# A transformer block on one core: value products of a head group in one burst, seven exponential buffers, three staging buffers

## The chip, the core and the metric
One core of a Trainium2 chip runs the whole program. The metric is the device time of one execution in microseconds. The kernel before takes 591.67 us (median of three runs: 591.47, 597.71, 591.67).

## The reference
Eight sequences of 512 tokens, 128 channels, float32. Layer 1, on the layer-normed x: RMS norm; q, k, v by three 128x128 products; q and k normalised per head (16 heads of 8 channels); scores with a relative-position bias that is constant beyond 128 positions; a causal softmax that excludes the diagonal; values; an output projection with residual; RMS norm; a two-layer ReLU network of 512 hidden units with residual. The result is layer-normed and added to x. Layer 2: layer norm, then eight experts of 352 hidden units, of which each token takes its two best, layer norm and residual.

```python
attn = jnp.einsum('bqhd,bkhd->bhqk', q, k) + bias
attn = attn * scale[None, :, None, None]
attn = jnp.where(causal[None, None], attn, -1000000.0)
attn = jax.nn.softmax(attn, axis=-1)
y = jnp.einsum('bhqk,bkhd->bqhd', attn, v).reshape(B, S, E)
y = y @ Wo + x
...
g = jnp.einsum('th,eih->tei', x, gate_w)
u = jnp.einsum('th,eih->tei', x, up_w)
y = jnp.einsum('tei,ehi,te->th', jax.nn.silu(g) * u, down_w, w_te)
```

## The kernel before
**Stages.** After a start of some 39 us the attention stage runs eight bodies, b = 0 to 7, one per sequence. Then the expert stage runs 71 tiles of 128 tokens (`step` of each engine), the first forty of them interleaved with the end of body 7's work ("bodies" 8 and 9), then a final normalisation.

**A body** has 20 score units, n = 0 to 19, in four groups g of four heads, five units u each. A unit computes transposed scores into one half of the two-part PSUM tile SC (lines 716 to 742): units 0 and 1 take the first key tile of two heads each, units 2 and 3 the second and fourth tile, unit 4 the third tile of four heads. ScalarE takes the exponential of a unit, 128x1024 (line 1015), into a buffer EB[u]. VectorE and GpSimd (POOL) multiply parts of it by an exponential bias table (lines 442 to 455 and 1363): VectorE units 0, 2 and 4, POOL units 1 and 3; in odd bodies from 3 on VectorE takes unit 1 too from the second group on (`takes`). TensorE then multiplies by the values, four heads side by side in 32 columns each, accumulating in the PSUM tile OA (line 748): `pv01` for units 0 and 1, `pv23` for 2 and 3, `pv4` for 4.

**Order.** Every engine works through its queue in the order of the program. That order is written by hand: the dictionaries PE_AT, ACT_AT, DVE_AT and POOL_AT (lines 43 to 50) say behind which unit n of a body a piece of other work is issued. Such work is, for the body ahead, the preparation of q, k, v (`pre_xt`, `pre_qk`, `pre_val`, `pre_turn`, `peel` on TensorE, with the copies `pre_copy` and `first_part` to `third_part` on ScalarE; negative entries lie in the body before the last), and for the body behind, `on_m1`: vsum, o0, o1, yt, wo, zt, h0 to h3, ffn, and the routing (rx, logits, and in odd bodies from 3 on count). These share two PSUM tiles in turn. In odd bodies VectorE runs the routing chain `top`, `second_best` in unit 3, `shares` in 5 and `place` in 6 (line 1446), which waits for count; in bodies 5 and 7 the slot table follows (`expert_tiles`, `past_starts`). POOL's scatters wait for `place`.

**Waits.** Scores of unit n wait for the exponential of unit n-2 (line 721). The value products of group g stand at these places of TensorE's order: `pv01(g)` behind the scores of the group's unit 4, `pv23(g)` behind those of unit 1 of the next group, `pv4(g)` behind those of its unit 2 (lines 962 to 969). The exponential of a unit waits until its buffer of the group before has been multiplied (lines 1012 to 1014).

**Weights.** Twenty lots of expert weights are loaded into seven staging buffers WST (which lie in the later gather buffers YSA, XGA and in WSX), transposed by TensorE (`weights`, line 852) and copied by ScalarE (line 438): lots 0 to 6 behind units 14 to 20 counted from the start of body 6, lots 7 to 19 behind units 3 to 15 of body 7. The load of lot i waits for the transposition of lot i-7 (line 527). On SyncE's queue lots 0 to 6 stand before body 7's stores of q and k, lots 7 to 10 before the loads of the second half of its q and k (lines 553 and 558), the rest behind these. The zero pads of the expert slots are made in XGA and WSX at the start and written out behind body 0's loads (line 578).

Of the kernel before, what the change touches and what calls it, by code (L numbers as in the profile page):

```python
# [71 lines left out]
def block_kernel(nc, x_d, ln1_d, wq_d, wk_d, wv_d, rel_d, scale_d, wo_d, ln2_d, w1_d, w2_d,  # L72
# [30 lines left out]
    with ExitStack() as ctx:  # L103
# [16 lines left out]
        EB = [arena[:, 17408 + 1024 * u:17408 + 1024 * (u + 1)] for u in range(UNITS)]  # L120
# [97 lines left out]
        WSX = sb("WSX", [P, 3 * 512])  # L218
# [223 lines left out]
        def mul_first(eng, g, u):  # L442
            e = EB[u].rearrange("p (j c) -> p j c", j=2)
# [6 lines left out]
        def mul_mid(eng, g, u):  # L450
            e = EB[2 + u].rearrange("p (j c) -> p j c", j=2)
# [42 lines left out]
        def _(sp):  # L494
# [87 lines left out]
            for i in range(NHI + 4, NWT):  # L582
                stage(i)
# [48 lines left out]
        def _(pe):  # L632
# [119 lines left out]
            def pv01(b, g):  # L752
# [8 lines left out]
                e = lambda q0, n: lambda j: EB[j // 2][:, 512 * (j % 2) + q0:512 * (j % 2) + q0 + n]  # L761
# [3 lines left out]
            def pv23(b, g):  # L765
# [3 lines left out]
                e = lambda c, n: lambda j: EB[2 + j // 2][:, 512 * (j % 2) + c:512 * (j % 2) + c + n]  # L769
# [487 lines left out]
        def _(dve):  # L1257
# [287 lines left out]
            for b in range(NB + 2):  # L1545
                at = DVE_AT[b >= NB]
                for n in positions(b):
# [50 lines left out]
                    if 1 <= b <= NB:  # L1598
# [110 lines left out]
        def _(pool):  # L1709
# [90 lines left out]
            for b in range(NB + 2):  # L1800
                at = POOL_AT[b >= NB]
                for n in positions(b):
                    g, u = divmod(n, UNITS)
                    if b < NB and (u == 3 or u == 1 and not takes(b, g)):
# [94 lines left out]
```

## Time and profile before

| | |
|---|---|
| median of three runs | 591.67 us |
| profiled execution | 596.4 us span; its own time is 597.71 us, the only one of the three above the span, so 1.3 us lie around it |
| attention stage (39 to 368 us) | 329 us |
| TensorE / VectorE / ScalarE / POOL busy | 532.1 / 375.9 / 395.4 / 349.7 us |
| mean granted TensorE clock | 0.977 |

Busy time is a share of the span and averages over stages with different limits. Matmuls are pipelined and their records overlap, so the steps between starts tell more than the sum of the durations. Where a line of the trace merges several instructions (x3), its start is that of the first.

### The profile page before, as it was taken

How to read it: one execution, taken by the hardware profiler on the slowest of the kernel's cores; microseconds unless marked ns; L12 is line 12 of the kernel's file. 1: busy time of each engine (PE TensorE's matmuls, PEld its weight loads, DVE VectorE, ACT ScalarE, POOL GpSimd, SP SyncE). 2: the span in 40 equal slices, each digit the busy share in tenths (PEclk: the TensorE clock that was granted, in tenths of full speed). 3: DMA queues.
4: the chain of work that ended last, by engine and by line, in shares of the span. 5: the costliest groups of instructions: out<-in, count | busy, mean ns of one | idle time of the engine just before them, and what ended most of it. 6: DMA issues, size and time to landing. Idle time of an engine off the chain costs nothing.

```text
span 596.4 us, 14609 instructions
## 1 busy us (share of the span) xinstructions
PE 532.1 (89%) x4952; PEld 395.0 (66%) x4969; DVE 375.9 (63%) x1095; ACT 395.4 (66%) x880; POOL 349.7 (59%) x449
## 2 busy tenths in 40 slices
PE   6989899899899899988899899999976899999981
PEld 5655455556566455655555666889976899999960
DVE  6824583965975947996847877527742365555347
ACT  3388989888978788869788696644531355555425
POOL 6104636545538885357877258487578555565545
PEclk9999999999999999999999999999996799999997
DMA  7245333213213322232734512212122203321174
GB/s 196 76 126 161 111 99 109 74 37 108 80 45 122 102 86 71 77 100 78 201 109 134 132 56 52 59 55 69 55 61 69 55 32 86 88 63 32 33 287 141
DMA packets 47016, 55.62 MB, mean 93 GB/s; under 512 B 7376, under 2 KB 41056, under 8 KB 44784
## 3 DMA queue, kind: packets, MB, share of 16 engines
q1 hardware_dynamic: 42624, 45.76, 26.7%
q0 software_dynamic: 4320, 8.92, 4.5%
q8 instruction: 42, 0.69, 0.5%
q14 instruction: 30, 0.25, 0.2%
HBM read 36.27 MB, written 18.92 MB: 93 GB/s over the span
## 4 chain that ended last, share of the span: by engine, by line
PE 56%; DVE 15%; ACT 10%; POOL 6%; issue 6%; DMA 3%; another core or an unknown queue 3%; DVEq 1%; SPq 0%; ACTq 0%; POOLq 0%
PE SC L871 11%; PE OA L748 9%; PE OA L881 6%; PE M L786 4%; PE M L822 4%; PE SC L730 3%; ACT arena L1015 3%; PE SC L734 2%; PE M L643 2%; DVE SS L1330 2%; PE SC L740 2%; PE M L662 1%; POOL slots L1782 1%; PE M L852 1%
## 5 line engine op out<-in xcount | busy, mean ns | idle before, releaser
L1015 ACT ACTIVATE arena<-SC 128x1024 f32<-128x1024 f32 x160 | 161.9, 1039 | 14.7 <-PE SC L735 11.8
L871 PE MATMUL SC<-arena 128*128 128x128 f32 (+1 forms) x852 | 111.5, 283 | 0.0
L871 PEld LDWEIGHTS SC<-arena 128*128 128x128 f32 (+1 forms) x852 | 104.0, 191 | 0.4 <-issue 0.3
L748 PE MATMUL OA<-arena 128*32 128x256 f32 (+1 forms) x1536 | 88.9, 349 | 6.6 <-DVE arena L455 2.8
L1782 POOL DMA_INDIRECT slots<-XBA,IDX x64 | 72.6, 1134 | 37.0 <-DVE IDX L1455 19.6
L1503 DVE TENSOR_TENSOR arena<-arena,SC 128x256 f32<-128x256 f32 (+1 forms) x142 | 43.7, 348 | 68.6 <-issue 24.6
L881 PE MATMUL OA<-arena 128*128 (+1 forms) x426 | 62.5, 284 | 12.9 <-issue 8.1
L748 PEld LDWEIGHTS OA<-arena 128*32 128x32 f32 x1536 | 39.2, 109 | 44.0 <-issue 22.8
L881 PEld LDWEIGHTS OA<-arena 128*128 128x128 f32 (+1 forms) x426 | 55.2, 198 | 15.4 <-issue 15.4
L454 POOL TENSOR_TENSOR arena<-arena 128x512 f32<-128x512 f32 x32 | 42.7, 1335 | 36.2 <-ACT arena L1015 35.6
L447 POOL TENSOR_TENSOR arena<-arena 128x512 f32<-128x512 f32 x23 | 31.2, 1356 | 48.9 <-ACT arena L1015 48.8
L1793 POOL DMA_INDIRECT ytok<-YSA,XGA x39 | 38.7, 993 | 34.0 <-ACT YSA L1118 28.3
L1112 ACT ACTIVATE arena<-SC 128x256 f32<-128x256 f32 (+1 forms) x142 | 38.6, 324 | 25.6 <-PE SC L871 16.6
L1363 DVE TENSOR_TENSOR arena<-arena 128x1024 f32<-128x1024 f32 x32 | 40.6, 1268 | 17.6 <-ACT arena L1015 17.6
L1511 DVE COPY arena<-arena 128x704 f32 x71 | 38.2, 538 | 16.6 <-issue 14.4
L1793 POOL DMA_INDIRECT ytok<-arena x32 | 32.0, 1001 | 27.4 <-ACT arena L1118 23.2
L447 DVE TENSOR_TENSOR arena<-arena 128x512 f32<-128x512 f32 x41 | 34.1, 833 | 18.8 <-ACT arena L1015 18.2
L734 PE MATMUL SC<-arena 72*128 72x384 bf16 x128 | 35.2, 329 | 6.9 <-ACT arena L1015 6.9
L730 PE MATMUL SC<-arena 72*128 72x512 bf16 x128 | 38.4, 381 | 2.9 <-ACT arena L1015 1.3
L1118 ACT ACTIVATE YSA<-OA,XGA 128x128 f32<-128x128 f32 x39 | 14.3, 367 | 36.4 <-PE OA L881 18.9
L454 DVE TENSOR_TENSOR arena<-arena 128x512 f32<-128x512 f32 x32 | 26.1, 816 | 18.3 <-ACT arena L1015 18.2
L1118 ACT ACTIVATE arena<-OA,arena 128x128 f32<-128x128 f32 x32 | 11.8, 367 | 33.0 <-PE OA L881 21.3
(244 smaller groups left out, 1086.0 us busy)
## 6 DMA issues: line engine op xcount, KB each, us to landing
arena<-parts SPq DMA_DIRECT2D x90, 192.0 KB
parts<-arena SPq DMA_DIRECT2D x16, 384.0 KB
arena<-ytok SPq DMA_DIRECT2D x8, 512.0 KB, 7.3
XGA<-slots SPq DMA_DIRECT2D x39, 65.0 KB
arena<-slots SPq DMA_DIRECT2D x32, 65.0 KB, 1.9
X<-in_L_attn_x SPq DMA_DIRECT2D x4, 512.0 KB, 5.1
out<-X SPq DMA_DIRECT2D x8, 256.0 KB, 2.5
arena<-parts SPq DMA_DIRECT2D x12, 96.0 KB
```

Source lines behind the costliest of these rows:

```text
L447: return eng.tensor_tensor(v, v, tab, ALU.mult)
L454: return [eng.tensor_tensor(a, a, TAB[:, h0:h0 + 3:2, P:3 * P], ALU.mult), eng.tensor_tensor(z, z, TAB[:, h0:h0 + 3:2, P:2 * P], ALU.mult)]
L730: mm = pe.matmul(s[:, 512 * i:512 * i + 512], KS[0:ROWS, h, 0:P], QS[0:ROWS, h, :], start=True, stop=True)
L734: pe.matmul(s[:, 512 * i:512 * i + 384], KS[0:ROWS, h, P:2 * P], QS[0:ROWS, h, P:4 * P], start=True, stop=True)
L748: mm = pe.matmul(OA[32 * j:32 * j + 32, q0:q0 + n], vals[:, t, 32 * h:32 * h + 32], probs(j), start=first, stop=last, skip_group_check=True)
L871: mm = pe.matmul(SC[0:n, r % 2, 512 * m + P * c:512 * m + P * (c + 1)], WSEL[s % 4][:, I * m + i0:I * m + i0 + n], XGT[r % 2], start=True, ...
L881: mm = pe.matmul(OA[:, 0:P], HTB[r % 2][0:n, P * c:P * (c + 1)], WALL[0:n, bass.ds(off + 2 * I + P * c, P)], start=c == 0, stop=c == NIC - 1)
L1015: act.activation(EB[u], SC[:, n % 2, :], ACT.Exp).then_inc(exp_done, 1)
L1363: dve.tensor_tensor(e, e, TAB[:, heads, P:3 * P], ALU.mult).then_inc(mul_dve, 1)
L1503: ins = dve.tensor_tensor(HTB[r % 2][0:k, c0:c1], SGB[r % 2][0:k, c0:c1], SC[0:k, r % 2, 512 + c0:512 + c1], ALU.mult)
L1782: pool.indirect_dma_start(out=slots_d.ap(), out_offset=bass.IndirectOffsetOnAxis(ap=IDX[b // 2 % 2][:, k, T * r + t:T * r + t + 1], axis=0 ...
L1793: pool.indirect_dma_start(out=ytok_d.ap(), out_offset=bass.IndirectOffsetOnAxis(ap=XG[r][:, D + 1:D + 2].bitcast(I32), axis=0), in_=YS[r], ...
```

## The change
- `pv01`, `pv23` and `pv4` of group g are issued one after the other, behind the scores of unit 1 of the next group. Only the last group of the last body keeps `pv01` behind its own unit 4, and the other two at the start of the expert stage.
- The exponentials go round a ring of seven buffers (the five of before, a new tile EBX, and YSA) instead of one buffer for each unit of a group. The wait names the unit that had the buffer seven exponentials ago.
- The first gather buffers move from XGA into WSX. Weight lots are staged in the three parts of WSX. On SyncE's queue lots 0 to 2 stand in the first place, 3 to 6 in the second, 7 to 19 in the third. The pads are made in XBA, and VectorE waits for their transfers before it first writes there.
- Places: val from 1 to 2 and qk0 from -4 to -3 on TensorE, qk0 from -5 to -3 on ScalarE, count from 6 to 7 on TensorE; place2, tab0 and tab1 from 6 to 7 on VectorE.

```diff
-PE_AT = (dict(val=1, turn0=4, turn1=8, xt=-5, qk0=-4, qk1=-2, ... count=6, peel00=5, peel01=6, peel10=9, peel11=10),
+PE_AT = (dict(val=2, turn0=4, turn1=8, xt=-5, qk0=-3, qk1=-2, ... count=7, peel00=5, peel01=6, peel10=9, peel11=10),
-ACT_AT = (dict(val=2, seed=1, xt=-6, qk0=-5, qk1=-2, ...
+ACT_AT = (dict(val=2, seed=1, xt=-6, qk0=-3, qk1=-2, ...
-DVE_AT = (dict(... place=5, place2=6, tab0=6, tab1=6, tab2=9, ln=16, xstat=16, xb=19),
+DVE_AT = (dict(... place=5, place2=7, tab0=7, tab1=7, tab2=9, ln=16, xstat=16, xb=19),
...
-        EB = [arena[:, 17408 + 1024 * u:17408 + 1024 * (u + 1)] for u in range(UNITS)]
...
-        XGA = sb("XGA", [P, INNER * ROW])
+        EBX = sb("EBX", [P, 1024])
         YSA = sb("YSA", [P, INNER * D])
+        EBR = [arena[:, 17408 + 1024 * u:17408 + 1024 * (u + 1)] for u in range(UNITS)] + [EBX[:, :], YSA[:, :]]
+        NEB = len(EBR)
+        WSX = sb("WSX", [P, 3 * 512])
+        XGA = WSX[:, 0:INNER * ROW]
...
-        WST = [a[:, 512 * k:512 * (k + 1)] for a, n in ((YSA, 2), (XGA, 2), (WSX, 3)) for k in range(n)]
+        WST = [WSX[:, 512 * k:512 * (k + 1)] for k in range(3)]
         NST = len(WST)
-        PADV = [a[:, 0:E * ROW].rearrange("p (e c) -> p e c", c=ROW) for a in (XGA, WSX)]
+        PADV = [XBA[:, r].rearrange("p t k c -> p (t k) c") for r in range(2)]
...
+        def eb(b, g, u):
+
+            return EBR[(NU * b + UNITS * g + u) % NEB]
...
                 if b == NB - 1:
                     sp.wait_ge(dummy_out, 32)
-                    for i in range(NHI):
+                    for i in range(NST):
                         stage(i)
...
                     if b == NB - 1 and half:
-                        for i in range(NHI, NHI + 4):
+                        for i in range(NST, NHI):
                             stage(i)
...
-            for i in range(NHI + 4, NWT):
+            for i in range(NHI, NWT):
                 stage(i)
...
                     before = (b, g - 1) if g else (b - 1, GROUPS - 1)
-                    if 0 <= before[0] < NB and (b < NB or before[0] == NB - 1 and b == NB and g == 0):
-                        if u == 1 and b < NB or n == 0 and b == NB:
-                            pv23(*before)
-                        if u == 2 and b < NB or n == 0 and b == NB:
-                            pv4(*before)
-                    if b < NB and u == 4:
+                    if b < NB and u == 1 and before[0] >= 0:
+                        pv01(*before)
+                    if b < NB and u == 1 and before[0] >= 0 or b == NB and n == 0:
+                        pv23(*before)
+                        pv4(*before)
+                    if b == NB - 1 and n == NU - 1:
                         pv01(b, g)
...
             def exp_unit(b, n):
-                u = n % UNITS
                 act.wait_ge(qk_done, NU * b + n + 1)
 
-                done = 3 * (GROUPS * b + n // UNITS) + (-2, -2, -1, -1, 0)[u]
-                if done > 0:
-                    act.wait_ge(pv_done, done)
-                act.activation(EB[u], SC[:, n % 2, :], ACT.Exp).then_inc(exp_done, 1)
+                old = NU * b + n - NEB
+                if old >= 0:
+                    act.wait_ge(pv_done, 3 * (old // UNITS) + (1, 1, 2, 2, 3)[old % UNITS])
+                act.activation(eb(b, *divmod(n, UNITS)), SC[:, n % 2, :], ACT.Exp).then_inc(exp_done, 1)
...
                         if n == at["xb"]:
                             dve.wait_ge(x1_rstd, c + 1)
-                            if c >= 2:
+                            if c < 2:
+                                dve.wait_ge(dummy_out, 32)
+                            else:
                                 dve.wait_ge(scattered[c % 2], 16 * 2 * T * (c // 2))
```

## Rows read from the trace of the kernel before

**Rows 1.** Stretches of the span: length, busy time of each engine, granted clock, DMA share.
```profile
39.00:368.40 329.40, 301.51 (x3078) 185.70 (x3093) 234.56 (x581) 274.93 (x494) 196.59 (x192) 1.00 0.33 98
```

**Rows 2.** The same view: body 2 and body 5.
```profile
113.00:153.00 40.00, 37.48 (x364) 22.97 (x366) 27.03 (x66) 35.13 (x63) 20.95 (x21) 1.00 0.25 80
237.90:282.30 44.40, 40.07 (x382) 24.89 (x384) 38.28 (x110) 35.14 (x65) 24.20 (x27) 1.00 0.26 84
```

**Rows 3.** Timeline of TensorE, body 2: start, duration, line, output from input, count.
```profile
137.61 0.64 PE L748 MATMUL OA<-arena 128*32 128x256 f32 x8
138.18 2.05 PE L786 MATMUL M<-W,H1T 128*128 128x128 f32 x16
...
142.88 1.07 PE L748 MATMUL OA<-arena 128*32 128x256 f32 x16
143.88 0.61 PE L730 MATMUL SC<-arena 72*128 72x512 bf16 x2
144.32 0.60 PE L643 MATMUL M<-IDN,arena 128*128 128x128 f32 x4
```

**Rows 4.** Timeline of TensorE at the start of the expert stage.
```profile
373.27 1.51 PE L748 MATMUL OA<-arena 128*32 128x256 f32 x32
374.71 0.66 PE L828 MATMUL M<-IDN,XBA 128*128 128x128 f32 x4
```

**Rows 5.** Timeline of ScalarE, body 4, units 10 to 13; in brackets idle time before.
```profile
218.73 1.02 ACT L1015 ACTIVATE arena<-SC 128x1024 f32<-128x1024 f32 x1
...
220.11 1.11 ACT L1102 ACTIVATE H1T<-M 128x512 f32<-128x512 f32 x2
221.10 1.04 ACT L1015 ACTIVATE arena<-SC 128x1024 f32<-128x1024 f32 x1
222.59 1.02 ACT L1015 ACTIVATE arena<-SC 128x1024 f32<-128x1024 f32 x1 [0.45 <-PE SC L735]
...
225.58 1.02 ACT L1015 ACTIVATE arena<-SC 128x1024 f32<-128x1024 f32 x1 [0.32 <-PE SC L735]
```

**Rows 6.** Timeline of ScalarE, exponentials around and in body 2.
```profile
112.06 2.93 ACT L1015 ACTIVATE arena<-SC 128x1024 f32<-128x1024 f32 x3
...
131.24 1.04 ACT L1015 ACTIVATE arena<-SC 128x1024 f32<-128x1024 f32 x1
...
143.16 1.01 ACT L1015 ACTIVATE arena<-SC 128x1024 f32<-128x1024 f32 x1
...
152.09 2.02 ACT L1015 ACTIVATE arena<-SC 128x1024 f32<-128x1024 f32 x2
```

**Rows 7.** Timelines of TensorE and VectorE, body 3, units 4 to 7.
```profile
164.46 0.60 PE L730 MATMUL SC<-arena 72*128 72x512 bf16 x2
164.98 1.08 PE L748 MATMUL OA<-arena 128*32 128x256 f32 x24
...
167.55 1.90 PE L838 MATMUL M<-MM,ONES 128*128 128x64 f32 x16
...
167.29 1.22 DVE L1363 TENSOR_TENSOR arena<-arena 128x1024 f32<-128x1024 f32 x1
```

**Rows 8.** Timelines of ScalarE and TensorE: idle times in bodies 4 and 5.
```profile
199.25 0.31 ACT L1044 ACTIVATE RSQ<-SS 128x128 f32<-128x128 f32 x1 [2.00 <-DVE SS L1332]
...
215.95 1.07 PE L748 MATMUL OA<-arena 128*32 128x256 f32 x16 [0.91 <-issue]
...
264.82 1.08 PE L748 MATMUL OA<-arena 128*32 128x256 f32 x24 [1.10 <-DVE arena L455]
```

**Rows 9.** SyncE's queue and TensorE at the start of body 7; landings of line 532.
```profile
323.17 2.08 SPq L553 DMA_DIRECT2D arena<-parts  x3
...
327.38 1.68 SPq L532 DMA_DIRECT2D WSX<-in_L_ffn_up_w  x3
...
331.85 0.60 PE L852 MATMUL M<-IDN,YSA 128*128 128x128 f32 x4
...
DMA to landing us min/median/max: 3.6/6.2/8.8
```

More of the change, by code:

```diff
@@ L37 @@
 RSQRT_SEED = float(0x5F3759DF)
-PE_AT = (dict(val=1, turn0=4, turn1=8, xt=-5, qk0=-4, qk1=-2, rx=3, logits=4, vsum=1, o0=3, o1=3, yt=5, wo=6, zt=7, h0=8, h1=9, h2=10, h3=10, ffn_a=12, ffn=13, count=6, peel00=5, peel01=6, peel10=9, peel11=10),
+PE_AT = (dict(val=2, turn0=4, turn1=8, xt=-5, qk0=-3, qk1=-2, rx=3, logits=4, vsum=1, o0=3, o1=3, yt=5, wo=6, zt=7, h0=8, h1=9, h2=10, h3=10, ffn_a=12, ffn=13, count=7, peel00=5, peel01=6, peel10=9, peel11=10),
     dict(rx=0, logits=1, vsum=0, count=3, o0=1, o1=2, yt=3, wo=5, zt=6, h0=7, h1=7, h2=7, h3=7, ffn_a=8, ffn=8))
-ACT_AT = (dict(val=2, seed=1, xt=-6, qk0=-5, qk1=-2, out0=12, out1=1, rx=2, rexp=6, yt=4, ysq=12, zt=7, h0=8, h1=9, h2=10, h3=10, xb2=3, part0=4, half0=4, last0=6, part1=8, half1=9, last1=10, xar=-7, xa=1),
+ACT_AT = (dict(val=2, seed=1, xt=-6, qk0=-3, qk1=-2, out0=12, out1=1, rx=2, rexp=6, yt=4, ysq=12, zt=7, h0=8, h1=9, h2=10, h3=10, xb2=3, part0=4, half0=4, last0=6, part1=8, half1=9, last1=10, xar=-7, xa=1),
     dict(out1=0, rx=0, xb2=2, rexp=3, yt=4, zt=6, ysq=6, h0=6, h1=6, h2=7, h3=7, xa=3))
-DVE_AT = (dict(norm0=-3, norm1=1, norm2=1, lg=2, top2=3, top2b=3, vsum=0, o0=1, o1=1, wo=4, ffn=13, astat=13, place=5, place2=6, tab0=6, tab1=6, tab2=9, ln=16, xstat=16, xb=19),
+DVE_AT = (dict(norm0=-3, norm1=1, norm2=1, lg=2, top2=3, top2b=3, vsum=0, o0=1, o1=1, wo=4, ffn=13, astat=13, place=5, place2=7, tab0=7, tab1=7, tab2=9, ln=16, xstat=16, xb=19),
     dict(lg=1, top2=1, top2b=2, vsum=0, place=3, place2=3, tab0=4, tab1=17, tab2=21, o0=1, o1=2, wo=5, ffn=8, astat=9, ln=12, xstat=13, xb=15))
@@ L209, in block_kernel @@
         SCM = sb("SCM", [P, 2, max(FIRST, EARLY - FIRST, STILES - EARLY), E])
-        XGA = sb("XGA", [P, INNER * ROW])
+        EBX = sb("EBX", [P, 1024])
         YSA = sb("YSA", [P, INNER * D])
+        EBR = [arena[:, 17408 + 1024 * u:17408 + 1024 * (u + 1)] for u in range(UNITS)] + [EBX[:, :], YSA[:, :]]
+        NEB = len(EBR)
+        assert INNER * D == 1024 and INNER * ROW <= 3 * 512
+        WSX = sb("WSX", [P, 3 * 512])
+        XGA = WSX[:, 0:INNER * ROW]
         XGB = arena[:, 8192:8192 + (RING - INNER) * ROW]
@@ L439, in copy_lot, with mul_first @@
             ins.then_inc(wt_free, 1)
-        def mul_first(eng, g, u):
-            e = EB[u].rearrange("p (j c) -> p j c", j=2)
+        def eb(b, g, u):
+            return EBR[(NU * b + UNITS * g + u) % NEB]
+        def mul_first(eng, b, g, u):
+            e = eb(b, g, u).rearrange("p (j c) -> p j c", j=2)
             h0 = col(g, 2 * u)
@@ L447, in mul_first, with mul_mid @@
             return eng.tensor_tensor(v, v, tab, ALU.mult)
-        def mul_mid(eng, g, u):
-            e = EB[2 + u].rearrange("p (j c) -> p j c", j=2)
+        def mul_mid(eng, b, g, u):
+            e = eb(b, g, 2 + u).rearrange("p (j c) -> p j c", j=2)
             h0 = col(g, 2 * u)
@@ L760, in pv01 @@
                     pe.wait_ge(o_out, 2 * b + g // 2)
-                e = lambda q0, n: lambda j: EB[j // 2][:, 512 * (j % 2) + q0:512 * (j % 2) + q0 + n]
+                e = lambda q0, n: lambda j: eb(b, g, j // 2)[:, 512 * (j % 2) + q0:512 * (j % 2) + q0 + n]
                 pv(b, g, V2[b % 2], 0, 0, 256, e(0, 256), first=g % 2 == 0)
@@ L768, in pv23 @@
                 pe.wait_ge(mul_pool, by_pool + 3 - takes(b, g))
-                e = lambda c, n: lambda j: EB[2 + j // 2][:, 512 * (j % 2) + c:512 * (j % 2) + c + n]
+                e = lambda c, n: lambda j: eb(b, g, 2 + j // 2)[:, 512 * (j % 2) + c:512 * (j % 2) + c + n]
                 pv(b, g, V2[b % 2], 1, 128, 256, e(0, 256))
@@ L775, in pv4 @@
                 pe.wait_ge(mul_dve, muls(b, g)[0] + 4 + takes(b, g))
-                e = lambda j: EB[4][:, 256 * j:256 * j + 256]
+                e = lambda j: eb(b, g, 4)[:, 256 * j:256 * j + 256]
                 pv(b, g, V2[b % 2], 2, 256, 256, e, last=g % 2 == 1).then_inc(pv_done, 1)
@@ L1356, in mul @@
                 if u < 2:
-                    mul_first(dve, g, u).then_inc(mul_dve, 1)
+                    mul_first(dve, b, g, u).then_inc(mul_dve, 1)
                 elif u == 2:
-                    for i in mul_mid(dve, g, 0):
+                    for i in mul_mid(dve, b, g, 0):
                         i.then_inc(mul_dve, 1)
                 elif u == 4:
-                    e = EB[4].rearrange("p (j c) -> p j c", j=4)
+                    e = eb(b, g, 4).rearrange("p (j c) -> p j c", j=4)
                     dve.tensor_tensor(e, e, TAB[:, heads, P:3 * P], ALU.mult).then_inc(mul_dve, 1)
@@ L1808, in _ @@
                         if u == 1:
-                            mul_first(pool, g, 1).then_inc(mul_pool, 1)
+                            mul_first(pool, b, g, 1).then_inc(mul_pool, 1)
                         else:
-                            for i in mul_mid(pool, g, 1):
+                            for i in mul_mid(pool, b, g, 1):
                                 i.then_inc(mul_pool, 1)
```

2 lines of the change are left out of this document (1 added, 1 removed).

## The prediction
> **What bounds the kernel now.** I read first the stretches of the whole span: the attention loop, eight bodies of twenty units from 39 to 368 us, takes 329 of the 596 us, and the expert stage behind it the last 228 [rows 1]. The diff touches the second stage only in where its buffers lie, so the argument is about the first. There the second reading, body by body, shows TensorE busy 37 to 40 us of a body's 40 to 44 and ScalarE 35; the granted clock is 1.00, the level of 2.4 GHz [rows 2]. Neither engine is full: they take turns. Scores n may not start before exponential n-2 is done (two score buffers), and exponential n waits for scores n. So I cut a body into slots, from one exponential to the next. A slot lasts as long as the longer of two chains: ScalarE's exponential and its copies of that slot, or what TensorE has between two score units.
>
> Third reading, the prices. On ScalarE a slot with an exponential and three copies is 218.73 to 221.10, 2.37 us, and the last two of the copies are 220.11 to 221.10, 0.99 [rows 5]: 0.5 a copy and 0.9 the exponential. On TensorE a score unit is 0.44 when something other than value products follows and 0.52 in front of them [rows 3, 7], so entering value products costs 0.08. First part (sixteen records) 1.00 to the next work, second part about the same (1.08 us of records for 1.07 [rows 3, 7]), third part 0.57 [rows 3]; the first streams twice the columns of the third, so 256 columns cost 0.43 and 0.14 of each is the leaving. The one place where second and third part already stand together takes 1.44 [rows 4] against 1.57 apart: the 0.13 of one exit. A burst of three is then 0.86+0.86+0.43+0.14 = 2.29 in place of 2.57, and two entries of 0.08 go as well: 0.45 us per group, 14 us of TensorE time over 32 groups. The Trainium skill (TensorE: Matmul & The Clock Gate, section Back-to-back issue gap) has matmuls follow each other at their column time plus a few ns; by that rule alone the burst would save none of it and each burst slot would be 0.4 longer. The rows show more than that between the pieces, and the sum goes by the rows.
>
> **Part 1, the burst, in a full body.** Where TensorE bounds a slot, its time moves with the products; where ScalarE does, it doesn't. For body 2, in slots (lengths before from the starts of its 21 exponentials, of which [rows 6] show the first, the tenth, the fifteenth and the last two; the first and the last stand within a row of several):
> - Slots 4 to 7: the first part leaves slot 4 (3.9 to 2.9); slot 6 gets two parts for one (1.7 to 3.0); the third part leaves slot 7 (1.7 to 1.4). 8.2 and 8.2.
> - Slots 9 to 13, 11.9 before: in slot 9 TensorE falls to 1.5, but ScalarE needs an exponential and two copies, 1.9 (2.6 before). Slot 10 has three copies, 2.4. In slot 11 TensorE goes from one score unit to the next in 0.52+2.29 = 2.8; ScalarE has one exponential to do and starves: 2.6 (1.5 before). Slot 12 falls from 3.0 to the 2.67 of ScalarE's own work (222.59 to 225.58 less 0.32 idle [rows 5]), slot 13 stays at 2.5. Sum 12.1.
> - Slots 14 to 19, 9.9 before: 1.5, 0.9, 2.2 (burst), 1.9, 2.3, 0.9, with the copies of qk0 now behind exponential 17. Sum 9.7.
> - Slots 0 to 3 and 8: 10.0 before, 10.0 after; slot 1 is ScalarE's 3.6.
> So a full body gains nothing: the 1.8 us of junctions saved are spent while ScalarE starves behind the burst. Bounds: -1.8 (all of it on the path) and +1.1 (one burst slot more without its give-back). I take 0 for body 2.
>
> **Bodies 0 and 1** have less TensorE work between scores, so a burst is not hidden. Body 0: slot 11 goes from 1.2 to 2.5 and slot 6 up by 1.2, of which 0.8 comes back: +1.7. Body 1: +0.5. Bounds -1 and +3 together. I take +2.2.
>
> **Part 2, odd bodies 3, 5, 7.** VectorE runs the routing chain (some fifteen small operations) in unit 3, ahead of unit 4's product, which therefore ends at 167.29+1.22 = 168.5 in body 3 [rows 7]. Before, the third part that needs it stood in slot 7 behind the second part, the peel, wo and the 1.9 us count. In the change it stands in slot 6: scores 6 begin 1.0 sooner (163.5), the first two parts end at 165.7, and TensorE waits 2.8 us. Queued behind the wait: peel01, wo, scores 7, then zt (which also waits for VectorE's 0.7 us addition behind wo), then count, which moved to slot 7 and no longer covers anything. Scores 8 come 2.7 us late; ScalarE and POOL, which waits for the scatter indices, idle meanwhile. Later slots return little: +2.2 in body 3 (bounds 0.8 and 2.9). Body 5 has now a wait of 1.10 us before its second part of group 1 [rows 8], on products that stood behind the slot table; in the change that product runs before the table: +1.0. Body 7 +1.2 by the same. Together +4.4, bounds 0 and +8.7.
>
> **Part 3, even bodies 4 and 6.** They now pay a 0.91 us wait before the first part of group 1 (its product on POOL is late from the scatters) and 2.00 us of ScalarE on VectorE's sums [rows 8]; slot 1 is 5.6 instead of 3.9 there. The first wait has two more slots of slack in the change; the second one shrinks as its products are needed later. -1.6 each, -3.2 together, bounds -5 and -0.6.
>
> **Part 4, staging.** Three buffers instead of seven. Lots 3 to 6 are asked for three lots ahead, about 5 us before use, and the shortest landing in the view of this line is 3.6 [rows 9]: I cost them at nothing; what hides it is the distance, and if it fails each late lot costs up to 1. But lots 7 to 9 now go out behind the last six loads of queries and keys. There three weight loads are issued from 327.38, behind loads that began at 323.17, and TensorE wants lot 7 at 331.85 [rows 9]. Issue to landing is 3.6 to 8.8 in this view, the 8.8 being one queued behind six such loads; so lot 7 is there between 331.4 and 336.6, a wait of 0 to 4.8. I take 335.2, nearer the upper end since it has the same queue before it: +3.4. Lots 8 and 9 arrive while it is made up for. Later lots have 5.6 us or more from one use to the next.
>
> **Edits with one answer.** The ring of seven: the exponential that would reuse a buffer of group g stands, by the score order, behind scores that stand behind the burst; its wait never ends last. The pads written from other tiles, the addresses of gather buffers, and VectorE's wait for the pads (done near 47 us, needed near 113) cost nothing. A last group of body 7 is laid out as before.
>
> **Sum.** 0 + 2.2 + 4.4 - 3.2 + 3.4 = +6.8 us. The profiled execution goes from a span of 596.4 to 603.2 (597.7 to 604.5 in its own time); it lies 6 us over the median, so against the median of 591.67 the sum gives 598.5.
>
> **Rivals.**
> - A, TensorE is the path nearly everywhere: then the 14 us come out, less 3.4 for the weights and some of the odd bodies' wait: -14+3.4+2.2 = about 583 to 587. For it: TensorE is busy over 90% of the stage [rows 1]. Against: slots 9 to 14 where ScalarE's copies already set the length. Chance 0.13.
> - B, it evens out: the odd bodies' wait is taken up by later slack (bounds 0) and the loads land within 4 us: 2.2-3.2+1 = 0, 590 to 595. For it: half of the waits that I add fall where the others have spare time. Chance 0.24.
> - C, plainly slower, by one mechanism: the wait for unit 4's product in slot 6. If nothing of it is given back in bodies 3, 5 and 7 (2.9 each) and the even bodies' waits stay (-0.6), the sum is 2.2+8.7-0.6+3.4 = +13.7, 605. It decides from the point where VectorE's chain ends over 2 us after scores 6. Chance 0.16.
> - The forecast, 594 to 602: 0.47.
>
> **Numbers.** 1% is 5.9 us, about what a measurement of this kernel tells from no change. Slower by more: C and two thirds of the forecast, 0.46. Within: 0.39, from the rest of the forecast and nearly all of B. Faster: 0.15. Range 587 to 606, which leaves out most of A and the far end of C.
>
> **What would show it.** Right: TensorE's value products as records of x48 of about 2.3 us; in bodies 3, 5, 7 an idle time before the last eight of them, released by VectorE's L1363; ScalarE idle before the exponential behind each burst; a transposition of weights waiting for a DMA some 8 us into body 7; bodies 3 and 7 longer, 4 and 6 shorter. Wrong: bodies 1 and 2 shorter by 1.5 us each, which would be rival A, or no wait at lot 7.

## The result, and the profile after

The changed kernel takes 626.06 us (median of four: 617.2 to 628.34) beside 593.57 of the kernel before in the same comparison: **1.047 of it, interval 1.037 to 1.057, so slower by 5%, some 28 us by that ratio**. Executions come in a quicker and a slower state, and the ratio counts only those in the quicker one (617.2 and 625.49 us here), to which the profiled execution below, 628.34 us, does not belong. Two later comparisons on other chips gave 1.056 (1.051 to 1.061) and 1.053 (1.046 to 1.060). The forecast was 598.5 us with a range of 587 to 606; the direction was right, the size not.

The profiled execution has a span of 626.6 us in a time of 628.34; the readings that the account rests on are held against a0 below, the same kernel, whose profiled execution took 626.11. By stretch (length; busy time of PE, PEld, DVE, ACT and POOL; granted clock, DMA share, GB/s), the attention stage, body 2, body 4 and the expert stage:

```profile
39.10:402.50 363.40, 308.54 (x3082) 199.66 (x3081) 237.18 (x578) 273.74 (x494) 199.41 (x190) 0.95 0.30 89
119.30:162.90 43.60, 38.22 (x366) 25.03 (x366) 28.15 (x66) 35.15 (x64) 23.77 (x21) 0.96 0.22 73
211.50:260.00 48.50, 39.71 (x366) 25.65 (x366) 28.49 (x67) 35.37 (x63) 33.06 (x30) 0.93 0.24 77
402.50:626.60 224.10, 196.05 (x1591) 183.17 (x1583) 120.25 (x397) 102.46 (x346) 144.86 (x229) 0.96 0.27 81
```

Against [rows 1, 2] the loss is in the attention stage, 363.4 us for 329.4 (the expert stage is 224.1 for 228.0), and it isn't work: ScalarE is busy 274 us of the stage as before, and a TensorE busy for 308 us includes matmuls at half speed. The granted clock, 1.00 in that stage before, is 0.95. Lengths of the bodies 0 to 7, from the first exponential of one to that of the next (the last to its own twentieth):

```
before    35.2 38.7 40.0 42.2 42.6 44.4 42.8 41.9   sum 327.9
changed   40.9 39.3 43.6 48.6 48.5 47.1 48.2 47.2   sum 363.4
a0        38.6 39.3 41.7 48.3 42.4 52.9 42.5 50.8   sum 356.6
forecast  b0+b1 +2.2, b2 0, odd from 3 +4.4, b4+b6 -3.2, staging +3.4
```

**Slot 1 of bodies 2 to 6.** Timelines of TensorE, VectorE and ScalarE, body 4 (start, duration; in brackets the idle time before and what ended it):

```profile
213.10 1.05 PE L756 MATMUL OA<-arena 128*32 128x256 f32 x24
216.53 0.64 PE L756 MATMUL OA<-arena 128*32 128x256 f32 x8 [2.38 <-DVE arena L1370]
...
217.45 0.50 PE L742 MATMUL SC<-arena 72*128 72x384 bf16 x1
...
218.28 2.02 PE L676 MATMUL M<-WQKV,arena 128*128 128x128 f32 x8
...
212.75 1.92 DVE L1337 TENSOR_REDUCE SS<-arena 128x128 f32<-128x1024 f32 x1
214.71 0.73 DVE L1339 TENSOR_SCALAR SS<-SS 128x128 f32<-128x128 f32 x1
215.26 1.21 DVE L1370 TENSOR_TENSOR arena<-arena 128x1024 f32<-128x1024 f32 x1
...
215.47 0.31 ACT L1051 ACTIVATE RSQ<-SS 128x128 f32<-128x128 f32 x1 [2.01 <-DVE SS L1339]
```

The burst's last four matmuls (the x8: each float32 matmul leaves two records) wait 2.38 us until VectorE has done unit 19's product, which stands in its queue behind the sums of squares (the same late sums for which ScalarE waits, as in [rows 8]). In bodies 2, 3, 5 and 6 the same wait is 1.92 us. Soon behind it, from 217.1, everything is slow for 3.4 us: scores of 0.50 for 0.34, the value matrix 2.02 where it takes 1.11 elsewhere. Granted clock there: 0.5, the level of 1.2 GHz. This does not follow each of these waits: in slot 1 it does in bodies 2, 4 and 6 and not in 3 and 5.

**The burst itself at that clock.** TensorE in slot 11 of body 0, and below it a burst at 2.4 GHz, slot 11 of body 4 (the answer to [rows 3, 4]):

```profile
59.62 0.41 PE L756 MATMUL OA<-EBX,arena 128*32 128x256 f32 x2
...
60.93 2.75 PE L756 MATMUL OA<-arena 128*32 128x256 f32 x32
...
242.40 1.94 PE L756 MATMUL OA<-arena 128*32 128x256 f32 x40
244.16 0.61 PE L756 MATMUL OA<-EBX,arena 128*32 128x256 f32 x8
244.71 0.34 PE L742 MATMUL SC<-arena 72*128 72x384 bf16 x1
```

From the burst's start to the next scores: 244.71 - 242.40 = 2.31 us (the prediction's price was 2.29), and 63.61 - 59.62 = 3.99 in the slow stretch.

**Slot 6 of body 3** has the wait that Part 2 forecast (answer to [rows 7]):

```profile
177.13 0.28 PE L756 MATMUL OA<-YSA,arena 128*32 128x128 f32 x2
...
179.88 1.08 PE L756 MATMUL OA<-arena 128*32 128x256 f32 x8 [2.45 <-DVE arena L1370]
180.89 0.61 PE L722 MATMUL M<-arena,NIB 128*128 128x512 bf16 x1
181.29 1.85 PE L821 MATMUL M<-WO,YT 128*128 128x128 f32 x8
```

2.45 us of idle time (forecast 2.8), and again what follows runs at half speed: four matmuls (x8) in 1.08 for 0.64.

**Slot 6 of body 4**, a body that was to shrink, is 5.9 us; 3.0 was the forecast for this slot of body 2 (TensorE, POOL, ScalarE):

```profile
230.18 0.22 PE L743 MATMUL SC<-arena 72*128 72x128 bf16 x1
233.80 0.77 PE L651 MATMUL M<-IDN,Y 128*128 128x128 f32 x4 [3.41 <-DVE Y L1393]
...
224.20 2.89 POOL L463 TENSOR_TENSOR YSA<-YSA,arena 128x256 f32<-128x256 f32 x1
227.25 1.01 POOL L1791 DMA_INDIRECT slots<-XBA,IDX  x1 [0.16 <-issue]
...
231.50 0.60 ACT L1096 ACTIVATE arena<-M 128x512 bf16<-128x512 f32 x1 [3.29 <-remote]
233.02 1.02 ACT L1022 ACTIVATE arena<-SC 128x1024 f32<-128x1024 f32 x1 [0.93 <-remote]
```

TensorE's records show slot 7's scores done at 230.4, but ScalarE's exponential of them starts at 233.02: the completions came 2.6 us late, while POOL issued four scatters from 227.25 on. **Lot 7** of the weights waits (answer to [rows 9]):

```profile
364.90 0.63 PE L860 MATMUL M<-IDN,WSX 128*128 128x128 f32 x4 [2.10 <-DMA WSX<-in_L_ffn_gate_w]
```

### The profile page after: what moved, and what is told of

Same layout as the page of the kernel before. It is cut to its first block, busy times and chain, and to the rows that moved or that the text cites. A ratio compares the mean times of both kernels' runs of the same rounds, so it can differ in the third digit from the quotient of the medians.

```text
span 626.6 us, 14626 instructions
## 1 busy us (share of the span) xinstructions
PE 536.3 (86%) x4969; PEld 405.1 (65%) x4969; DVE 380.1 (61%) x1095; ACT 395.1 (63%) x880; POOL 356.2 (57%) x449
## 4 chain that ended last, share of the span: by engine, by line
PE 45%; DVE 23%; POOL 8%; ACT 7%; issue 6%; another core or an unknown queue 4%; DMA 4%; SPq 1%; DVEq 1%; ACTq 0%; POOLq 0%
PE SC L879 12%; PE OA L756 6%; PE OA L889 6%; PE M L830 3%; DVE SS L1337 2%; POOL slots L1791 2%; POOL RZ L1775 2%; PE M L794 2%; PE SC L742 2%; DVE A L1617 2%; ACT arena L1022 2%; PE SC L738 1%; DVE STP L1406 1%; DVE arena L1370 1%
## 5 line engine op out<-in xcount | busy, mean ns | idle before, releaser
L1022 ACT ACTIVATE arena<-SC 128x1024 f32<-128x1024 f32 x115 | 117.6, 1040 | 25.3 <-PE SC L743 21.8
L879 PE MATMUL SC<-arena 128*128 128x128 f32 (+1 forms) x852 | 108.0, 277 | 0.0
L879 PEld LDWEIGHTS SC<-arena 128*128 128x128 f32 (+1 forms) x852 | 100.6, 186 | 0.4 <-issue 0.3
L756 PE MATMUL OA<-arena 128*32 128x256 f32 (+1 forms) x1104 | 69.7, 362 | 13.4 <-DVE arena L1370 12.5
L1802 POOL DMA_INDIRECT ytok<-YSA,WSX x39 | 39.1, 1002 | 33.8 <-ACT YSA L1125 27.5
L462 POOL TENSOR_TENSOR arena<-arena 128x512 f32<-128x512 f32 x23 | 29.3, 1275 | 49.1 <-ACT arena L1022 49.0
L1518 DVE COPY arena<-arena 128x704 f32 x71 | 38.3, 539 | 16.1 <-issue 14.3
L1370 DVE TENSOR_TENSOR arena<-arena 128x1024 f32<-128x1024 f32 x23 | 32.2, 1400 | 16.0 <-ACT arena L1022 16.0
L455 POOL TENSOR_TENSOR arena<-arena 128x512 f32<-128x512 f32 x17 | 21.9, 1290 | 28.1 <-ACT arena L1022 27.9
L1796 POOL MEMSET IDLE<- 128x128 f32 x103 | 24.7, 240 | 16.9 <-DVE IDX L1462 16.7
L1125 ACT ACTIVATE YSA<-OA,WSX 128x128 f32<-128x128 f32 x39 | 14.3, 367 | 30.7 <-PE OA L889 19.8
L830 PE MATMUL M<-ZT,W 128*128 128x512 f32 x64 | 33.0, 624 | 0.0
```

What stands on the lines that cost most here:

```text
L756: mm = pe.matmul(OA[32 * j:32 * j + 32, q0:q0 + n], vals[:, t, 32 * h:32 * h + 32], probs(j), start=first, stop=last, skip_group_check=True)
L830: mm = pe.matmul(M1[:, :], W1[:, P * c:P * (c + 1)], ZT[:, :], start=True, stop=True)
L879: mm = pe.matmul(SC[0:n, r % 2, 512 * m + P * c:512 * m + P * (c + 1)], WSEL[s % 4][:, I * m + i0:I * m + i0 + n], XGT[r % 2], start=True, ...
L1022: act.activation(eb(b, *divmod(n, UNITS)), SC[:, n % 2, :], ACT.Exp).then_inc(exp_done, 1)
L1370: dve.tensor_tensor(e, e, TAB[:, heads, P:3 * P], ALU.mult).then_inc(mul_dve, 1)
L1802: pool.indirect_dma_start(out=ytok_d.ap(), out_offset=bass.IndirectOffsetOnAxis(ap=XG[r][:, D + 1:D + 2].bitcast(I32), axis=0), in_=YS[r], ...
```

## The experiments

Ratios are to the kernel before, run beside, with 95% intervals. The four groups of runs were on different chips, so differences in us are taken within one group alone. "Slot" lengths come from each trace as above.

### First group: which part costs (kernel before 582.25 us)

**e1**, the places of before in the changed kernel:
```diff
-PE_AT val=2, qk0=-3, count=7; ACT_AT qk0=-3; DVE_AT place2=7, tab0=7, tab1=7
+PE_AT val=1, qk0=-4, count=6; ACT_AT qk0=-5; DVE_AT place2=6, tab0=6, tab1=6
```


> The changed kernel with the places of before (val 1, qk0 -4 and -5, count, place2, tab0, tab1 at 6). Theory P (the loss is the burst: its last eight products stand one unit too early for VectorE's product of unit 4, and the granted clock falls in the waits): the burst keeps nearly all of the loss, 618 to 630. Theory Q (the loss is the moved places, which put VectorE's sums of squares ahead of the product of unit 19): most of the loss goes, 595 to 608, and slot 1 of bodies 2 to 6 falls from 5.1 to 6.1 us to under 4.

617.27 us, 1.060 (1.053 to 1.068). Theory Q falls: with the old places the burst is no cheaper. Slot 1 of body 4 is 8.3 us, slot 6 of body 3 8.9, slot 15 4.5 in bodies 1 to 5 for 0.9 in the changed kernel (2.9 before). The new places take these waits away, but the whole time does not show a gain by them: 1.060 lies within the intervals of the changed kernel's ratios.

**e2**, the third part back behind unit 2:
```diff
-                        pv4(*before)
+                    if b < NB and u == 2 and before[0] >= 0 or b == NB and n == 0:
+                        pv4(*before)
```


> The changed kernel, but pv4 alone goes back behind the scores of unit 2; pv01 and pv23 stay together behind those of unit 1. Theory P: the wait for unit 4's product in slots 1, 6, 11, 16 goes with it, 597 to 608, slot 6 of bodies 4 and 6 back under 4 us, and the granted clock of the attention stage near 1.00. Theory Q: the third part waits in slot 2 as long as it waited in slot 1, 618 to 630.

596.02 us, 1.022 (1.015 to 1.030). Slot 6 of bodies 4 and 6 is 2.6. The changed kernel has 1.047 to 1.056: more than half of the loss hangs on four matmuls per group standing one unit earlier. (Slot 1 stays 5.1: see e4.)

**e4**, changed kernel with the products where they stood before:
```diff
+                        if u == 1 and b < NB or n == 0 and b == NB:
+                            pv23(*before)
+                        if u == 2 and b < NB or n == 0 and b == NB:
+                            pv4(*before)
+                    if b < NB and u == 4:
+                        pv01(b, g)
```


> The changed kernel with the value products where they stood before (pv01 behind unit 4, pv23 behind 1, pv4 behind 2); ring, staging and the new places stay. Theory P: 592 to 600. Theory Q: 608 to 625, with the wait for the product of unit 19 now in slot 2.

593.92 us, 1.015 (1.006 to 1.025). Theory P is the nearer one (1.015 is at the upper end of its 592 to 600 us, held against the kernel before), with a surprise: TensorE waits for unit 19's product behind scores 2 as well, and slot 1 is 5.0 to 5.3 us where 3.9 was in bodies 2, 3 and 5. Body 2 (ScalarE, then TensorE):

```profile
113.53 1.02 ACT L1022 ACTIVATE YSA<-SC 128x1024 f32<-128x1024 f32 x1
116.00 0.31 ACT L1051 ACTIVATE RSQ<-SS 128x128 f32<-128x128 f32 x1 [1.46 <-DVE SS L1339]
...
117.16 0.88 PE L756 MATMUL OA<-arena 128*32 128x256 f32 x8 [2.12 <-DVE arena L1370]
```

So it is the moved places that make VectorE's sums late, by 1.2 us in three bodies. The sums don't wait for the moved copies themselves, which end at 111.7; they start at 113.01, behind a product of VectorE that took 1.42 and 0.94 us beside POOL's, for 0.95 and 0.41 before. Which of the places does it was not run alone. They give time back elsewhere (body 1: 38.3 for 38.7).

**e5**, of the change only ring and staging (e4 with the old places):

> The kernel before with nothing of the change but the ring of seven buffers and the three staging buffers (with what they need: pads in XBA, gather buffers in WSX). Both theories: the ring costs nothing. The prediction's Part 4 gives +3.4 us for the staging (bounds 0 and 4.8), so 595 to 598 beside a kernel before of 592 to 594; the wait of the weights for their loads that the changed kernel's trace shows (2.1 us in all) gives +2.

592.08 us, 1.018 (1.011 to 1.025). From body 0 to the start of body 7 it takes 285.5 us, as before to 0.5 us: **the ring costs nothing**. Body 7 is 51.8 for 41.9. SyncE's queue and TensorE there, and the stretch of body 7:

```profile
323.06 2.08 SPq L561 DMA_DIRECT2D arena<-parts  x3
325.18 2.05 SPq L566 DMA_DIRECT2D arena<-parts  x3
327.27 8.90 SPq L540 DMA_DIRECT2D WSX<-in_L_ffn_gate_w  x4
...
334.69 1.09 PE L860 MATMUL M<-IDN,WSX 128*128 128x128 f32 x4 [2.78 <-DMA WSX<-in_L_ffn_gate_w]
335.57 1.06 PE L748 MATMUL SC<-arena 72*128 72x256 bf16 x4
...
340.15 1.10 PE L860 MATMUL M<-IDN,WSX 128*128 128x128 f32 x4
```
```profile
324.98:376.74 51.76, 46.37 (x388) 30.11 (x392) 31.97 (x94) 33.63 (x74) 22.77 (x30) 0.84 0.34 86
```

Lot 7 lands at 334.7, inside the forecast 331.4 to 336.6, and the wait is 2.8 us (forecast 3.4). But behind it the clock is 0.5 for 17 us: a lot takes 1.09 us for 0.60 in [rows 9], and 2.8 us of wait become 9.8 us of body, where 2 to 3.4 were expected.

### Second group: the three waits (kernel before 597.58 us)

**a0**, the changed kernel again.

> The changed kernel as it is, once more, so that the others of this call have it on their own chip. If the stalls of slot 6 in bodies 4 and 6 (5.9 and 5.8 us) belong to the kernel, they are here again; if they belonged to that one execution or chip, slot 6 is about 3.3 there as in body 2, and the kernel comes nearer to 1.035 of the kernel before.

632.5 us, 1.056 (1.051 to 1.061). Slot 6 of bodies 4 and 6 is 3.0: the stall belongs to an execution, not to the order of the work alone. It isn't faster for it: in body 5 the clock was low for 10.2 us behind the wait of slot 6 (body 5 52.9 us). The waits are those of the changed kernel, but where the clock falls differs: behind slot 1 in body 5 alone, behind slot 6 in bodies 3 and 5.

**f1**, sixteen matmuls ahead of `pv4` in seven waits (f2: four):
```diff
                         pv23(*before)
+                        if 2 <= b < NB - 1 and (n == 1 or n == 6 and b % 2):
+                            pe.wait_ge(exp_done, NU * b + n)
+                            keep_busy(16, SC[:, (n + 1) % 2, :])
                         pv4(*before)
```


> The changed kernel with sixteen matmuls of 256 columns (about 1.7 us, into the half of SC whose exponential is done, overwritten by the next scores) ahead of pv4 in slot 1 of bodies 2 to 6 and in slot 6 of bodies 3 and 5, where TensorE waits for VectorE's product of unit 4 for 2.4 us and more. Theory K (a good part of the loss is the granted clock that falls to 0.5 behind those waits): TensorE does more, and the kernel is 4 to 10 us faster than the changed kernel, with slots 2 of bodies 2 to 6 back from 2.3 to 3.8 us to 1.9. Theory P (only the wait itself costs): no faster, same within 2 us, or slower by a few.

665.64 us, 1.113: inconclusive, since my price was wrong. One took 0.43 us, not the 0.11 that I had read off the value products; those run four side by side in 32 columns each. The slots became 10.2 us. Slot 2 of bodies 2 to 6 is 2.3 with the clock at 1.00, not the 1.9 expected. Repeated as f2 below.

**s1**, scatters `sc6` and `sc7` six units later in bodies 4 and 6:
```diff
- if n + NU * (b - body) == POOL_AT[body >= NB][f"sc{k}"]:
+ if n + NU * (b - body) == POOL_AT[body >= NB][f"sc{k}"] + (6 if body < NB - 1 and k >= 6 else 0):
```


> The changed kernel with POOL's last four scatters of each pair (sc6 and sc7) moved six units later in bodies 4 and 6. Theory S (those scatters hold up TensorE and POOL's products in slot 6): slot 6 of bodies 4 and 6 falls from 5.9 and 5.8 us to about 3.3, 4 to 6 us in all. Rival (the stall is POOL's product of unit 3, which took 2.89 us beside VectorE's): slot 6 stays above 5.

633.98 us, 1.062 (1.057 to 1.068), no gain. Slot 6 is 3.0 there, which says little (a0 has that too), but slot 11 of both bodies is 6.8 where 2.8 stands in the others: a stall stands where the scatters were moved to. TensorE, ScalarE and POOL, body 4:

```profile
234.48 0.22 PE L743 MATMUL SC<-arena 72*128 72x128 bf16 x1
...
238.73 1.02 ACT L1022 ACTIVATE arena<-SC 128x1024 f32<-128x1024 f32 x1 [5.67 <-remote]
...
232.54 1.01 POOL L1791 DMA_INDIRECT slots<-XBA,IDX  x1 [0.16 <-issue]
...
236.38 0.96 POOL L1791 DMA_INDIRECT slots<-XBA,IDX  x1 [0.30 <-issue]
```

The scores of TensorE's record are done at 234.7, the exponential that waits for them starts at 238.73, as POOL's four scatters end. That four scatters beside a burst can hold back what TensorE reports is shown by this move; by what path is open. It takes more than this company: in body 4 of h2 and in bodies 4 and 6 of e1 the four begin 0.1 us behind the start of slot 6, as in the changed kernel, and the slot is 3.3.

**n2**, the sums behind unit 19's product, seeds and roots one unit later:
```diff
-DVE_AT norm0=-3, norm1=1, norm2=1; ACT_AT seed=1
+DVE_AT norm0=-1, norm1=2, norm2=2; ACT_AT seed=2
```


> The changed kernel with VectorE's sums of squares behind unit 19's product instead of ahead of it (norm0 -1), and the root seeds and roots that need them one unit later (seed, norm1, norm2 at 2). Theory P: TensorE's wait for unit 19's product in slot 1 of bodies 2 to 6 goes (2.4 us and more each), slot 1 falls from 5.1 to 6.1 us to 3.6 to 4, and what the clock lost behind it comes back: 8 to 14 us faster than the changed kernel. Rival (ScalarE's wait for the sums sets slot 1 and only moves to slot 2): within 3 us of the changed kernel.

657.21 us, 1.101 (1.095 to 1.107). Both theories missed. Slot 1 does fall to 3.0 us, so the sums were what held up slot 1. But on VectorE the roots now stand behind the posts of `o0` and `o1`, which wait for TensorE's slot 3, and the transposition of slot 4 waits for the roots: slot 4 is 9.4 to 12.1 us. TensorE, body 2:

```profile
138.06 1.09 PE L683 MATMUL M<-IDN,arena 128*128 128x128 f32 x4 [5.26 <-DVE arena L1357]
```

### Third group: repairs (kernel before 579.45 us)

**f2**, f1 with fewer matmuls:
```diff
-                            keep_busy(16, SC[:, (n + 1) % 2, :])
+                            keep_busy(4, SC[:, (n + 1) % 2, :])
```


> As f1_idle_filled with four matmuls in place of sixteen. In f1 one took 0.43 us and not 0.11, so sixteen outlasted the wait by 4.5 us each; four are 1.7 us and end inside it. Theory K (the clock that falls behind these waits is a good part of the loss): the granted clock of bodies 2 to 6 stays at 1.00 nearly throughout, and the kernel is 4 to 10 us faster than the changed kernel, 1.035 to 1.05 of the kernel before. Theory P (the wait alone costs): the same as the changed kernel, 1.047 to 1.056.

603.51 us, 1.040 (1.037 to 1.043). The granted clock is 1.00 in bodies 1 to 6; the changed kernel wasn't in this group, so the worth of the four matmuls is read from the fourth.

**h1**, e5 with three lots earlier on SyncE's queue:
```diff
-                        for i in range(NST, NHI):
+                        for i in range(NST, NHI + 3):
...
-            for i in range(NHI, NWT):
+            for i in range(NHI + 3, NWT):
```


> e5_ring_and_staging with lots 7 to 9 on SyncE's queue ahead of the second half of body 7's queries and keys, not behind it. Theory W (all that ring and staging cost is lot 7's late landing, 2.8 us of wait, and the fallen clock behind it): slots 3, 4 and 6 of body 7 back to 1.9, 4.2 and 4.5 us, and 0.998 to 1.004 of the kernel before. Rival (three buffers are too few for what is between a use and the next at any place): lots 10 and 11 wait in their place, 1.01 and more.

580.83 us, 1.002 (1.000 to 1.004). Slots 3 and 4 are 1.9 and 4.1 again. Theory W holds for the time. Body 7 is still 45.0 for 41.9, slot 6 of it 6.9, with the clock at 0.5 for 6.8 us behind an idle time of 1.23; the kernel before has that idle time in the same place, and its clock stayed at 1.00.

**h2**, the same move in the changed kernel:

> The changed kernel with the same move of lots 7 to 9. Theory W: 5 to 9 us faster than the changed kernel (its body 7 is 47 to 51 us and goes to 42 to 44), 1.035 to 1.047 of the kernel before; the loss of the burst stays. Rival: no better.

601.56 us, 1.036 (1.033 to 1.039); body 7 is 42.5 us. W holds.

**h3**, h1 with `pv23` at unit 2 too:
```diff
-                        if u == 1 and b < NB or n == 0 and b == NB:
+                        if u == 2 and b < NB or n == 0 and b == NB:
                             pv23(*before)
```


> h1 with the second part one unit later, so that second and third part run together behind the scores of unit 2 and the first part stays behind unit 4: one junction and one entering fewer per group (0.2 us by the prediction's prices), and no product asked for earlier than before. If TensorE is the path nearly everywhere (the prediction's rival A), 0.985 to 0.992 of the kernel before; if ScalarE's copies set most slots (the prediction's reading), 0.995 to 1.005.

586.26 us, 1.007 (1.004 to 1.010): 0.7% slower, far from rival A's range and just above the other, into which the interval reaches. In the profiled execution bodies 0 and 1 are 0.7 and 1.1 us shorter, but slot 4 of bodies 2, 3 and 5 is 5.9 for 3.9. VectorE and POOL, body 2, of h3, and VectorE's same work in h1:

```profile
118.72 3.05 DVE L1357 TENSOR_TENSOR arena<-arena,RSQ 128x256 f32<-128x256 f32 x4
...
119.16 1.47 POOL L462 TENSOR_TENSOR arena<-arena 128x512 f32<-128x512 f32 x1 [3.36 <-ACT arena L1022]
...
121.91 0.63 PE L683 MATMUL M<-IDN,arena 128*128 128x128 f32 x4 [1.60 <-DVE arena L1357]
```
```profile
119.50 1.43 DVE L1357 TENSOR_TENSOR arena<-arena,RSQ 128x256 f32<-128x256 f32 x4
```

The earlier scores let POOL's product begin beside VectorE's four multiplications, which then take 3.05 us for 1.43. The Trainium skill (SBUF — State Buffer, section Who interferes with whom) says that a VectorE instruction with two inputs in SBUF and a GpSimd instruction that reads SBUF block each other. The trace agrees, here and where POOL's 0.72 became 2.89 beside VectorE's products in body 4 of the changed kernel. The profiled execution of h3 took 591.85 us and the shortest of its twelve 580.7; whether the shorter ones have this too no trace shows.

### Fourth group: the ladder (kernel before 594.02 us)

m1 is the changed kernel, m2 the kernel of f2, m3 both repairs, m4 is e2 with the lots earlier.

> The changed kernel, as the measure for the other three of this call: 1.045 to 1.056 of the kernel before.

> The kernel of f2 (four matmuls in each of seven waits). Theory K: faster than m1 by 4 to 10 us, and no stretch of granted clock 0.5 in bodies 2 to 6. If the wait alone costs: the same as m1 within 2 us.

> m2 and the lots 7 to 9 earlier, as in h2. If clock and staging are separate losses they add: 9 to 17 us faster than m1, 1.022 to 1.032 of the kernel before, and what is left is the wait for the products of unit 4 in slots 1 and 6.

> e2 (third part behind unit 2) and the lots earlier. e2 was 1.022 and the staging 1.018 on one chip, so 1.000 to 1.008 of the kernel before: the junctions that are saved bring nothing and cost nothing. Under 0.995 would speak for the prediction's rival A.

```
m1 changed                     625.23 us   1.053 (1.046 to 1.060)
m2 four matmuls in seven waits 614.76 us   1.036 (1.030 to 1.042)
m3 and lots 7 to 9 earlier     608.27 us   1.026 (1.020 to 1.032)
m4 third part at unit 2, lots  600.87 us   1.015 (1.009 to 1.020)
```

As theory K and the sum of the two losses had it (10.5 for 4 to 10, 17.0 for 9 to 17), but m4 is 0.7% over its bound. Bodies 2 to 6 as one stretch, m1, a0 and m2:

```profile
117.69:353.37 235.68, 197.02 (x1876) 129.03 (x1876) 163.16 (x400) 175.51 (x316) 138.53 (x130) 0.96 0.28 84
```
```profile
117.15:345.02 227.87, 193.14 (x1864) 128.81 (x1876) 172.71 (x400) 174.98 (x316) 136.98 (x130) 0.96 0.28 87
```
```profile
117.04:337.24 220.20, 201.19 (x1932) 132.75 (x1932) 173.86 (x400) 174.88 (x315) 136.14 (x130) 1.00 0.29 90
```

and m2's TensorE in slot 1 of body 4:

```profile
208.58 1.99 PE L657 MATMUL SC<-IDN 128*128 128x256 f32 x8
211.03 0.64 PE L756 MATMUL OA<-arena 128*32 128x256 f32 x8 [0.46 <-DVE arena L1373]
```

TensorE does 28 matmuls more in m2 (56 records) and the stretch is 15.5 us shorter than in m1, with the clock at 1.00. The late products are as late as before; only the idle time is gone. But m1's profiled execution, 634.0 us, has slot 6's stall (bodies 4 and 6 are 48.5 and 48.2 for 42.4 and 42.1 in m2), and a0 is without it (42.4 and 42.5) with nothing filled. Against a0's 227.9, or 228.1 in h2, the clock alone is worth 7.7 to 7.9 us. f2 and m3 have 220.3 and 220.2, as m2.

## Why the prediction was wrong

The comparison that shows its steps alone is m3, where the waits are there but neither the clock nor lot 7 adds to them (but for 3.4 us of clock 0.5 in body 0):

```
              b0+b1   b2           odd 3,5,7   b4+b6     staging    sum
forecast      +2.2    0            +4.4        -3.2      +3.4       +6.8
bounds        -1..+3  -1.8..+1.1   0..+8.7     -5..-0.6  0..+4.8
m3            +4.0    +1.7         +7.9        -1.0       -         +12.6
a0            +4.0    +1.7         +14.7 *     -0.6      +8.9       +28.7
changed       +6.3    +3.6         +9.1 *      +11.2     +5.2       +35.4
* bodies 3 and 5; all that body 7 is longer stands under staging
```

- **The step that cost most: "the granted clock is 1.00" [rows 2] was carried over to the kernel after**, as if it were a property of the stage; the sum has no term for it. Before, TensorE's longest idle time in bodies 1 to 6 is 1.35 us and the clock never falls there. The change puts seven waits of 1.9 to 2.5 us into bodies 2 to 6, and the clock fell behind four of them in the changed kernel's trace and behind three in a0. The engine then works at 1.2 GHz; where that meets a burst, it is 3.99 us for 2.31. Filling the seven is worth 10.5 us by the medians of m1 and m2, 9.9 by their ratios. The Trainium skill (TensorE: Matmul & The Clock Gate, section HAM oscillation — how this bites in real kernels) describes a kernel that waits for a DMA before each tile and finds the clock down each time. e5 agrees (2.78 us of wait for lot 7, then 0.5 for 17 us); the waits for VectorE agree in part, since the clock fell behind some and not behind others.
- **Part 1, a step missed:** "slot 1 is ScalarE's 3.6". It is 5.1 in bodies 2, 3 and 5, for 3.9 before. The moved places make VectorE's sums 1.2 us late (e4), and behind the sums stands unit 19's product, which the burst now asks for in slot 1, ahead of scores 2: slot 2 is 2.3 for 1.9 (a0 against e2). The two give +1.55 us in each of the three bodies, nearly all of body 2's +1.7. The prediction followed the product of unit 4 through slot 6 and not the same product, of the last group, through slot 1 of the next body: a queue that the diff moved past and that wasn't walked.
- **Bodies 0 and 1:** +4.0 for +2.2. Body 1 is right (+0.6 for +0.5), body 0 is +3.4 for +1.7; slot 16, a burst, is 3.8 there for 0.9 before, with the clock at 0.5.
- **Part 2, about right:** of the +7.9 in m3, 3.1 are slots 1 and 2 of bodies 3 and 5, which is Part 1's error. The 4.8 left stand beside the forecast's 4.4: 3.4 in body 3 (over its bound of 2.9), 0.9 in body 5, 0.5 in body 7.
- **Part 3 had the right sign and was mis-sized:** -1.0 in m3 for -3.2. The wait before the first part of group 1 went as forecast (slot 9 is 1.5 us shorter in both bodies), but ScalarE's wait for the sums did not shrink: slot 1 stays 5.6 in body 4 and is 5.1 in body 6. The +11.2 of the changed kernel's trace are the clock and the stall beside the scatters.
- **Part 4:** the wait was 2.8 for 3.4. Its cost is 9.8 us alone (e5), 6.5 by m2 and m3, since the clock falls behind it.
- **Right:** that the burst gives nothing back in a full body. Its price (2.31 for 2.29), ScalarE starving behind it (slot 11 of body 2 is 2.8 for 2.6, slot 16 is 2.2 as forecast), the wait for unit 4's product in slot 6 of the odd bodies by VectorE's routing chain (2.45 for 2.8), and the ring at nothing. Rival A has the runs against it: slots 9 to 19 of body 2 hold two bursts and no wait, and in m3 they are 0.16 us shorter than before, not the 0.90 of the junctions; and h3, which saves half of the junctions and asks for nothing earlier, isn't faster than the kernel before.
- **Rival C** has 10.3 without its staging term, nearer to m3's 12.6 than the forecast's 3.4. That is in part luck: it has the excess in slot 6 of the odd bodies, and most of it was in slots 1 and 2 and in the even bodies' wait.

The sum in the fourth group, by the medians: 31.2 us = 10.5 for the clock behind seven waits and what follows on it, 6.5 for the lots, 14.2 left in m3 (by the ratios 9.9, 6.1 and 15.4). How much of the 10.5 is the stall in m1's executions is open, as only one of them was traced. Open stays too why the clock falls behind one wait and not behind the next of the same length, why four scatters hold TensorE back in some executions, 3 to 4 us each time, and why m4 is at 1.015 and not at 1.008.

No version ran faster than the kernel before: h1 is level with it.

## What to carry to other kernels

Count a new wait on TensorE twice: its own length, and the work behind it at half the clock, which came behind about half of the waits here; if it can't be removed, a few throwaway matmuls inside it are nearly free (m2's slots 1 are as long as a0's). Before moving products earlier, walk the queue of the engine that makes them at every place where they will be asked for, the last group of a loop body included: here four of a group's twenty-four matmuls, one unit too early, cost more than the 14 us that all junctions could have saved (m1 to m4 is 24.4 us, 17.9 without the lots). Fewer staging buffers shift loads to another place of the queue; here, with the first of them put ahead of the long loads, they cost 0.2% (h1).

## What the runs showed of the chip

- TensorE's granted clock fell to 0.5 behind idle times of 1.9 to 2.8 us, but not behind each: behind 4, 3, 4, 5 and 2 of the seven waits in the traces of the changed kernel, a0, m1, h2 and s1. In body 0 of the changed kernel it fell behind shorter ones (the last two 0.58 and 0.42), in h1 behind 1.23 where the kernel before has the same idle time and no fall. With the seven filled, the longest that is left being 1.23, it stayed at 1.00 for 276 us (m2).
- Four matmuls of 32 columns each, side by side, take what one of 128 columns takes: 0.43 us for 256 columns of float32.
- Beside POOL's four scatters, what waited for TensorE started up to 4 us after its records' ends (234.7 to 238.7): in the executions of the changed kernel, m1, f1 and s1. In a0, f2, m2 and m3 one of the four had started before slot 6 and there is no stall; in e1 and in body 4 of h2 the four begin 0.1 us behind the start of slot 6, as in the changed kernel, and there is none either.
